# Attention's tail behind the last scores in an order of its own on free score banks; the first expert weights loaded in four column parts

## What is computed

```
x = x + mamba(layernorm(x))                      # selective scan, not changed
q, k, v = rope(norm @ Wq + bq), ctx @ Wk + bk, ctx @ Wv + bv    # 16 heads of 16, 77 keys
x = x + softmax(q k / 4) v @ Wo + bo
p = softmax(xn2 @ gate_w)                        # xn2 = layernorm(x), 8 experts
w, sel = top_k(p, 2); w = w / sum(w)
out = sum over chosen e of w_e * (up * gelu(gate)) @ down_w[e]   # gate, up = xn2 @ gate_up_w[e]
x = x + out
```

## Time and profile before

| | us |
|---|---|
| median of 3 runs | 2060.79 |
| lowest, highest | 2059.44, 2063.51 |
| the profiled execution | 2057.14 |
| its span, first to last instruction | 2055.0 |
| last scores to first gate_up matmul | 1203.5 to 1290.5 |
| expert phase from there | 764.5 |

### The profile page before, as it was taken

How to read it: one execution, slowest core, us unless ns; L and a number is a source line. 1 busy time by engine, 2 the same in 40 slices (tenths; PEclk the granted TensorE clock), 3 DMA queues, 4 the chain that set the end, 5 groups by cost and what they waited for, 6 DMA issues and landing times.

```text
span 2055.0 us, 29468 instructions
## 1 busy us (share of the span) xinstructions
PE 1867.7 (91%) x10630; PEld 1519.3 (74%) x10630; DVE 1165.8 (57%) x1760; ACT 1101.3 (54%) x2157; POOL 1099.4 (53%) x806
## 2 busy tenths in 40 slices
PE   5889999989898988878999982999999999999998
PEld 2667676767676867766666651788888888888897
DVE  4899998999999998975677753111111111111111
ACT  3898989898989998935767660111111111111111
POOL 1687878777877877844658854222222322222131
PEclk8999999999999999999999995899999999999999
DMA  4121211121121114001111013944444343444441
GB/s 118 35 63 42 63 52 63 52 58 57 44 71 42 63 43 124 18 21 46 32 42 42 26 59 110 380 137 127 127 113 144 108 149 106 125 129 110 139 152 16
DMA packets 98131, 177.21 MB, mean 86 GB/s; under 512 B 24211, under 2 KB 68627, under 8 KB 87732
## 3 DMA queue, kind: packets, MB, share of 16 engines
q1 hardware_dynamic: 82308, 156.63, 22.7%
q0 software_dynamic: 15680, 18.69, 5.5%
HBM read 152.81 MB, written 22.82 MB: 85 GB/s over the span
## 4 chain that ended last, share of the span: by engine, by line
PE 49%; ACT 4%; DVE 3%; POOL 1%; issue 1%; DMA 1%; POOLq 0%; SPq 0%; DVEq 0%; ACTq 0%
PE e_ps L1643 24%; PE e_ps L1656 12%; PE m_ps L1417 3%; PE m_ps L1347 2%; PE m_ps L1392 2%; PE m_ps L1403 1%; ACT t_probs L1005 1%; PE m_ps L1340 1%; ACT m_a_ring L369 1%; PE m_ps L1333 1%; PE e_ps L1630 1%; ACT m_bxT L381 1%; PE m_ps L684 1%; POOL slots L953 1%; PE m_ps L593 1%
## 5 line engine op out<-in xcount | busy, mean ns | idle before, releaser
L324 POOL TENSOR_TENSOR m_hc_ring<-m_h_ring,m_c_bc 128x1024 f32<-128x1024 f32 x256 | 606.0, 2373 | 128.4 <-DVE m_h_ring L485 110.1
L1643 PE MATMUL e_ps<-e_xT,e_w 128*128 128x256 f32 (+1 forms) x2560 | 501.6, 357 | 0.8 <-ACT e_xT L1571 0.8
L1643 PEld LDWEIGHTS e_ps<-e_xT,e_w 128*128 128x128 f32 x2560 | 441.3, 191 | 51.5 <-issue 1.1
L1555 POOL DMA_INDIRECT out<-e_y,e_who x71 | 113.3, 1596 | 556.4 <-DVE e_y L1607 459.2
L576 PEld LDWEIGHTS m_ps<-m_ident,m_bxT 128*128 128x128 f32 x2048 | 234.9, 141 | 216.5 <-DVE m_h_ring L485 103.3
L369 ACT ACTIVATE m_a_ring<-m_delta,m_negA 128x512 f32<-128x512 f32 x512 | 366.3, 716 | 39.6 <-DVE m_h_ring L485 39.2
L576 PE MATMUL m_ps<-m_ident,m_bxT 128*128 128x128 f32 x2048 | 320.7, 280 | 67.6 <-DVE m_h_ring L485 61.7
L381 ACT ACTIVATE m_bxT<-m_uT,m_bT 128x512 f32<-128x512 f32 x512 | 364.6, 712 | 0.0
L1598 DVE TENSOR_TENSOR e_hT<-e_gact,e_ps 128x512 f32<-128x512 f32 x142 | 97.6, 687 | 459.7 <-ACT e_gact L1580 459.7
L485 DVE TENSOR_TENSOR_SCAN m_h_ring<-m_a_ring,m_carry,m_ps 128x512 f32<-128x512 f32 x256 | 317.4, 1271 | 27.6 <-ACT m_a_ring L369 13.5
L485 DVE TENSOR_TENSOR_SCAN m_h_ring<-m_a_ring,m_ps 128x512 f32<-128x512 f32 x256 | 304.3, 1210 | 35.7 <-ACT m_a_ring L369 12.4
(11 more groups left out here) (192 smaller groups left out, 2070.2 us busy)
## 6 DMA issues: line engine op xcount, KB each, us to landing
e_w<-in_gate_up_w SPq DMA_DIRECT2D x80, 1024.0 KB, 6.8
m_c_bc<-c_rows SPq DMA_DIRECT2D x32, 1024.0 KB, 5.9
e_w<-in_down_w SPq DMA_DIRECT2D x8, 1024.0 KB, 8.1
m_x_in<-in_x SPq DMA_DIRECT2D x8, 512.0 KB, 5.6
m_x_res<-in_x SPq DMA_DIRECT2D x8, 512.0 KB, 6.8
x<-m_x_res SPq DMA_DIRECT2D x8, 512.0 KB, 2.9
t_xa<-x SPq DMA_DIRECT2D x8, 512.0 KB, 4.6
out<-t_xa SPq DMA_DIRECT2D x8, 512.0 KB, 2.9
```

The costliest lines, as they stand in the source:

```text
L324: p.tensor_tensor(hc_ring[:, k % HC, :, :], h_ring[:, n % 2, e:e + 2, :], c_bc[:, n, :].unsqueeze(1).to_broadcast([P, 2, CT]), ALU.mult).t ...
L1555: nc.gpsimd.indirect_dma_start(out=out, out_offset=bass.IndirectOffsetOnAxis(ap=who[:, tile:tile + 1], axis=0), in_=y[:, s % 2, i, :], in_ ...
L1643: last = t.matmul(gu_bank(s, g, which)[:, f * wide:(f + 1) * wide], w1[s % W1_RING][:, c, lo:lo + P], xT[:, s % 2, c, 0:wide], start=(c == ...
```

## The change

There are three edits.

1. Slots 64 to 95 are gone. In their place each engine has a function `drain`, called once, which lists the rest of attention in a written order. C5, C6, C7 are the last three chunks, L the last half. Jobs no longer share the job bank there: the last half's O goes to bank 0, OUT(7) to banks 1 and 5, NT to banks 2 and 3, LG(6) to bank 4, LG(7) to bank 1, RK(6) and RK(7) to banks 6 and 7. New semaphores `late_nt`, `late_out`, `late_lg` count their emptying.
2. On DVE the sums of the last two tiles are made one slot earlier, at the slot's head.
3. `W1_AHEAD` is gone. SP loads of the first weights only the columns of group 0 when `tables` is there (two DMAs of 128 x 2 x 256, in runs of 1 KB), and the three other groups and then step 1 after the first gather has landed. PE waits for each part in front of its group.

```diff
+        def drain():
+            normalise(TOTAL - 1)
+            for n in range(TOTAL - SCATTER_AT - C5 * HT + HT, 2 * TI):
+                scatter(C5 - 1, n)
+            for c in (C5, C6, C7):
+                for n in range(2 * TI):
+                    scatter(c, n)
...
+        def norm_turned(c, i):
+            act.wait_ge(nt_done, KD * c + i + 1)
+            if i == 0:
+                act.wait_ge(lg_done, c)
+            a.activation(xn2T[:, i, :], ps[:, LATE_NT_BANK[c][i], :], ACT.Copy).then_inc(late_nt, 1)
+
+        def drain():
+            L = HALVES - 1
+            turned(L - 1, 4)
+            head_out(L - 1)
+            turned(L, 0)
+            root(rstd2, ln2, log2, C6, rstd2_ready)
+            turned(L, 1)
+            gap_root(C5)
+            turned(L, 2)
+            normed(C6)
+            turned(L, 3)
+            turned(L, 4)
+            head_out(L)
+            norm_turned(C6, 0)
+            norm_turned(C6, 1)
+            root(rstd2, ln2, log2, C7, rstd2_ready)
+            normed(C7)
+            norm_turned(C7, 0)
+            gap_root(C6)
+            norm_turned(C7, 1)
+            gap_root(C7)
...
+        def drain():
+            shift(C6, nmr2, mv2, rstd2, rstd2_ready, nmr2_ready)
+            choose(C5, 2)
+            choose(C5, 3)
+            share_out(C5)
+            place(C5)
+            projected(C7, 0)
+            projected(C7, 1)
+            dve.wait_ge(late_out, 2)
+            measured(C7)
+            logits(C6)
+            choose(C6, 0)
+            shift(C7, nmr2, mv2, rstd2, rstd2_ready, nmr2_ready)
+            for part in range(1, 4):
+                choose(C6, part)
+            share_out(C6)
+            place(C6)
+            logits(C7)
+            for part in range(4):
+                choose(C7, part)
+            share_out(C7)
+            place(C7)
+            list_steps()
...
-            if 0 <= g - 1 < TOTAL:
+            if 0 <= g - 1 < TOTAL - 2:
                 recip(g - 1)
             if 0 <= g + 1 < TOTAL:
                 maxima(g + 1)
+            if g >= TOTAL - 2:
+                recip(g)
...
+        def late_nt_job(c, i):
+            pe.wait_ge(xn2_ready, TI * c + TI)
+            if c == C6:
+                pe.wait_ge(exp_done, TOTAL)
+            else:
+                pe.wait_ge(late_nt, 2 - i)
+            turned(lambda j: xn2s[:, c % 2, j, i * P:(i + 1) * P], nt_done, ps[:, LATE_NT_BANK[c][i], :])
...
+        def drain():
+            L = HALVES - 1
+            turn(L - 1, 4)
+            times_v(L - 1, 3)
+            times_v(L - 1, 4)
+            turn(L, 0)
+            turn(L, 1)
+            times_v(L, 0)
+            job("RK", C5, 0)
+            turn(L, 2)
+            times_v(L, 1)
+            turn(L, 3)
+            times_v(L, 2)
+            turn(L, 4)
+            times_v(L, 3)
+            times_v(L, 4)
+            late_nt_job(C6, 0)
+            late_out_job(0)
+            late_out_job(1)
+            late_nt_job(C6, 1)
+            late_lg_job(C6)
+            late_nt_job(C7, 0)
+            late_nt_job(C7, 1)
+            pe.wait_ge(tr_evac, UNITS * HALVES)
+            ranks(C6)
+            late_lg_job(C7)
+            ranks(C7)
...
         sp.wait_ge(tabled, 3)
-        for r in range(W1_AHEAD):
-            weights.load_w1(sp, r)
+        weights.load_w1_part(sp, 0)
         sp.wait_ge(blanked, 16 * 3)
...
+    def load_w1_part(sp, g):
+        e = sp.value_load(tables[0:1, 0, 0:1], min_val=0, max_val=E - 1)
+        n = F2 // 2 // W1_PARTS
+        for c in range(KD):
+            sp.dma_start(
+                w1[0][:, c, :].rearrange("p (w f) -> p w f", w=2)[:, :, g * n:(g + 1) * n],
+                gate_up_w[bass.ds(e, 1), c * P:(c + 1) * P, :].rearrange("a p (w f) -> (a p) w f", w=2)[:, :, g * n:(g + 1) * n]
+            ).then_inc(w1_part[g], 16)
...
             for s in range(STEPS):
-                if s >= W1_AHEAD:
+                if s == 0:
+                    sp.wait_ge(x_loaded[0], 16 * loads_of[0])
+                    for g in range(1, W1_PARTS):
+                        weights.load_w1_part(sp, g)
+                else:
                     if s >= W1_RING:
                         sp.wait_ge(gu_done, first_group[s - W1_RING + 1])
                     weights.load_w1(sp, s)
...
-                pe.wait_ge(w1_loaded[s % W1_RING], 16 * KD * (s // W1_RING + 1))
+                if s:
+                    pe.wait_ge(w1_loaded[s % W1_RING], 16 * KD * w1_loads_of[s])
+                else:
+                    pe.wait_ge(w1_part[0], 16 * KD)
                 pe.wait_ge(xT_ready, s + 1)
                 gate_up(s, 0)
...
                 for g in range(1, groups_of[s]):
+                    if s == 0:
+                        pe.wait_ge(w1_part[g], 16 * KD)
                     gate_up(s, g)
```

More of the change, by code:

```diff
@@ L1248, in list_steps, with measured, projected, logits @@
             v.tensor_scalar(tables[:, 2, :], eid[:], 16.0, 16.0, ALU.mult, ALU.add).then_inc(tabled, 1)
+        def measured(c):
+            for i in range(TI):
+                measure(c, i, stats2, ln2)
+            spread(c, stats2, mv2, rstd2, ln2)
+        def projected(c, i):
+            dve.wait_ge(out_done, 2 * c + i + 1)
+            dve.wait_ge(bo_added, c + 1)
+            x = xa[c % X_RING][:, 2 * i:2 * i + 2, :]
+            v.tensor_tensor(x, ps[:, LATE_OUT_BANK[i], :].rearrange("p (i d) -> p i d", d=DM), x,
+                            ALU.add).then_inc(late_out, 1)
+        def logits(c):
+            dve.wait_ge(lg_done, c + 1)
+            v.tensor_copy(lg[:].rearrange("p e i -> p i e"),
+                          ps[:, LATE_LG_BANK[c], 0:TI * E].rearrange("p (i e) -> p i e", e=E)).then_inc(late_lg, 1)
+        def drain():
[21 more added lines that the diff above has]
+            list_steps()
         def slot(g):
+            if g == TOTAL:
+                return drain()
             c, q = g // HT, g % HT
@@ L1295, in slot @@
                 wait_emptied(dve, "OUT", c - 1, 1)
-                for i in range(TI):
-                    measure(c - 1, i, stats2, ln2)
-                spread(c - 1, stats2, mv2, rstd2, ln2)
+                measured(c - 1)
             for part in range(4):
@@ L1346, in projected, with logits, ranks @@
                 for m in range(KD):
-                    last = t.matmul(job_bank[:, n * DM:(n + 1) * DM], src(m)[:, tile * P:(tile + 1) * P],
+                    last = t.matmul(bank[:, n * DM:(n + 1) * DM], src(m)[:, tile * P:(tile + 1) * P],
                                     w[:, m, :], start=(m == 0), stop=(m == KD - 1))
             last.then_inc(done, 1)
+        def logits(bank):
+            for j in range(TI):
+                for m in range(KD):
+                    last = t.matmul(bank[:, j * E:(j + 1) * E], xn2T[:, m, j * P:(j + 1) * P], gw_sb[:, m, :],
+                                    start=(m == 0), stop=(m == KD - 1))
+            last.then_inc(lg_done, 1)
+        def ranks(c):
+            pe.wait_ge(chosen, c + 1)
+            bank, flat = rank_bank(c), upto[:].rearrange("p e i -> p (e i)")
+            t.matmul(bank[:, 0:E * TI], rank_w[:, 1, :], flat, start=True, stop=False)
+            t.matmul(bank[:, 0:E * TI], rank_w[:, 0, :], both[:].rearrange("p e i -> p (e i)"),
+                     start=False, stop=True)
+            t.matmul(bank[:, E * TI:E * TI + E], rank_w[:, 1, :], upto[:, :, TI - 1],
+                     start=True, stop=True).then_inc(rk_done, 1)
         def job(kind, c, i):
@@ L1370, in job @@
                 wait_emptied(pe, "NT", c, 1)
[L1371 to L1383 removed]
+                logits(job_bank)
+            if kind == "RK":
+                ranks(c)
         def scores(g):
@@ L1457, in expert_weights @@
     w1_loaded = [sem(f"e_w1_loaded{i}") for i in range(W1_RING)]
+    w1_part = [sem(f"e_w1_part{i}") for i in range(W1_PARTS)]
     w2_loaded = sem("e_w2_loaded")
```

106 lines of the change are left out of this document (68 added, 38 removed).

## The result

The changed kernel takes 2039.12 us (median of 4 runs, 2037.27 to 2042.75) against 2060.11 (2058.39 to 2063.51) beside it on the same chip: ratio 0.9898, 95% interval 0.9879 to 0.9918, some 21 us or 1.0% faster. A repeat gave 2042.44 and 2059.96, ratio 0.991 (0.9896 to 0.9923). The profiled execution has a span of 2038.0 us (before 2055.0) and an own time of 2040.1 (before 2057.14). The gain between the two profiled executions is thus 17.0 us, and it can be followed row by row. One execution of the kernel before, beside the later runs e10 and e7, was in a slower state (2097.63 us) and is left out everywhere.

The account below looks back on a forecast made before the run. PE works without a gap for the last 765 us, so the chain of waits up to the first gate_up matmul counts. 12.0 + 4.05 + 0.6 + 2.9 = 19.6 us off 2060.8 gives 2041.2, range 2036.5 to 2049.5.

Parts of the forecast that it names:

- k: Later weight parts and step 1's weights, now issued late: arrive before PE needs them, cost nil, bounds 0 and 3 us.
- rival of two steps at half speed: First expert steps: waits for weight parts keep PE at 1.2 GHz, two steps give 2084 us; chance 0.02.
- a to d: Attention tail: last normalise 3.9 us earlier, transposes 2.1, last half's O copied out 8.2, OUT(7) 9.3.
- b: Transposes of half 15: PE, busy with products until 1212.4, starts them only 2.1 us earlier.
- c: Last half's sets and products: despite PE waits of 1.2 and 0.7 us, O is copied out 8.2 us earlier.
- e: LG(6) ahead of chunk 7's shift: costs 1.4 us, shift at 1230.5, ACT's normalise ends 9.5 us earlier.
- f: NT(7) to RK(6): separate banks cut 3.57 us to 0.9 to 1.8; `place(6)` 12.0 us earlier, bounds 8 and 13.
- g: Sixteen Pool scatters: same 1.27 us each, nothing added, so the last one starts 12.0 us earlier, at 1256.0.
- h: Last scatter's landing: 2.7 us instead of 6.75 without the 4 MB of loads; gain 4.05 us, bounds 3.5 and 4.5.
- i: Meta load and barrier: Pool starts 4.65 us after the load instead of 5.3; gain 0.6 us, bounds 0 and 0.9.
- j: First gather of tokens: lands without weight loads beside it, instead of 5.85 us; gain 2.9 us, bounds 2 and 3.1.
- rival of small parts one after another: First weight parts: six loads each take their own 2.7 us, w1(1) some 8 us late, 2049 us; chance 0.05.

Follow-up runs that it names:

- e10: Changed kernel with VectorE's shift of chunk 7 ahead of chunk 6's logits and part 0 of the weights loaded behind the barrier: 2036.10 us, ratio 0.9898.
- e7: As e10, plus ScalarE's square root for chunk 6 ahead of its copy of O: 2035.82 us, ratio 0.9896.
- e3: Changed kernel with the second edit undone, VectorE summing the last two probability tiles at their slots' ends: 2045.66 us, single run.
- e1: Changed kernel's new attention tail, but weights of steps 0 and 1 loaded as before (four 1 MB DMAs): 2045.27 us, ratio 0.9933 to the kernel before.
- e4: Changed kernel with part 0 of the first weights loaded behind the barrier, not ahead of the wait for the scatters: 2037.46 us, ratio 0.9898.
- e8: Changed kernel without parts: step 0's two 1 MB loads ahead of the records, step 1's behind the first gather: 2040.25 us, ratio 0.9911.
- e5: Changed kernel with VectorE's shift for chunk 7 ahead of the copy of chunk 6's logits and first choose step: 2039.02 us, single run.
- e9: Changed kernel with both sets of chunk 7's transposes put through one bank: 2039.76 us, single run.
- e2: Attention tail of the kernel before, with the first expert weights in four parts: 2050.85 us, ratio 0.9963 to the kernel before.
- e6: Changed kernel with ScalarE's square root for chunk 6 ahead of its copy-out of half 14's O: 2039.02 us, single run.

## Why the prediction was right, and where not

2041.2 was forecast with a range of 2036.5 to 2049.5, and 2039.12 came. On the axis of the profiled execution 2037.5 was forecast and 2040.1 came, 2.6 us of gain less. That the median agrees better is luck: the medians' difference was 21.0 us once and 17.5 in the repeat. By the prediction's own signs of being wrong it is a near thing: the last scatter starts 10.9 us earlier, where 11 to 13 was asked, and lands in about 5.1 us, where anything over 5 was to count against it. The sum of the lower bounds there (13.5) leaves out the 3 us that *k* allows; with them it is 10.5. The rival of two steps at half speed adds to 2083, not 2084. Step by step:

- *a to d* hold to 0.2 us (to 0.3 counted from the last scores, which start 0.25 us earlier in this trace): last normalise 1209.19 (forecast 1209.4), transposes 1212.22 (1212.4), RK(5) 1215.74 (1215.8), last product ended 1222.15 (1222.1), OUT(7) 1226.55 (1226.5). But the working of *b* leaves out nearly half of what the second edit brings. By e3 (one trace) the earlier sums are worth 2.06 us directly and 1.8 more while PE keeps 2.4 GHz. The text took full speed from c on, which came true, and argued from the 2.85 us stop of before; but it gave no price to the second edit's part in keeping that stop short.
- *e*: the shift came at 1231.10, forecast 1230.5. 0.45 of that is this execution's: in e1, e4 and e8 it stands at 28.62 from the last scores, here at 29.07, since ACT copied NT(6,1) 0.26 us behind PE instead of 0.04 and LG(6) took 2.13 us instead of 1.92. LG(6) ahead of the shift cost 1.0 (e5), forecast 1.4.
- *f*: `place(6)` ended at 1237.62, forecast 1236.7, 11.1 us earlier instead of 12.0. The level did fall, though ahead of the stop that was to bring it, and the slow case came: RK(6) 1.76 us behind NT(7), where 0.9 to 1.8 was given and the middle taken. e9 confirms what the banks are worth.
- *g*: from the end of `place(6)` to the last scatter 19.5 us, before 19.35. Right.
- *h* is the step that failed: "issued at about 1253, and is gone before". It was issued from 1256.45, beside the scatter, and instead of 4.05 us the term gave 1.69. e4 shows that the mechanism was right: with nothing beside it the scatter lands in about 2.8 us. The time of issue was wrong twice. `tables` is there at 1254.0, not at 1252, since `place(7)` ends at 1245.8 and not at 1244; and SP took 2.5 us from there to its first issue, where the text had 1, and 2.9 for the two DMAs. Nor would the part have been gone: where it was issued 2.1 to 2.5 us ahead of the last scatter (e2, e3, e9) it took 4.4 to 5.2 us to land, and the way from scatter to meta load was 5.60, 4.30 and 4.00 us, against 3.2 to 3.6 with nothing there. The Trainium skill's rule cited there ("DMA: Bandwidth & Descriptors", Queues, rings and completion order: turns packet by packet), read as a protection of the scatter, isn't borne out: about 2.8 us of landing with nothing on SP's queue (e4), 3.2 to 5.1 with 0.5 MB (e9 and after the ends), 6.3 with 2 MB (e8), 6.8 and 7.0 with 4 MB (before, e1).
- *i* gave 0.94 (forecast 0.6), *j* 2.88 (2.9), *k* nothing, as forecast. For the third edit that is 5.5 us, and e2 alone gave 5.71.
- Not in the sum, and not the change's: the first 16 gate_up matmuls took 0.57 us less, since the level rose earlier in them. In the two repeats it is the other way round (5.32 before, 5.96 after).
- The rival of small parts one after another didn't come: the six parts, issued 1.2 us apart, landed in 2.9 to 3.5 us each, and step 1's two loads behind them in 5.1 to 7.1. The Trainium skill's rule that goes with it ("DMA: Bandwidth & Descriptors", Bandwidth: 1 MiB or more; the fixed cost of about 2 us stands in its section Anatomy of one DMA — SWDGE (gpsimd) path) had w1(1) at about 1295, an estimate. That would have stopped PE at 1290.2, where step 1 begins (48 of 64 matmuls of 13.81 us behind 1279.82). There is no such wait.

## What to carry to other kernels

In these runs a short transfer on the critical path paid for the loads in flight beside it, though they were on another queue: place big loads by when they are in flight, and read when they are really issued, not when their wait is satisfied. In a tail the banks of finished work are free, and here one emptying taken out of a chain of short steps was worth 1.0 us (e9). An idle time of PE can cost twice, once as such and once through the clock behind it (2.06 and 1.8 us in e3); read the granted clock behind each stop, since a fall also came without a long one.

## What the runs showed of the hardware that was not expected

- Issuing is not free for strided pieces: six part loads of 128 x 2 x 256 with their register work took SP 5.8 to 7.15 us, 1.0 to 1.2 each. Two whole loads of 128 x 2048 took 0.87.
- An order of issues can move by itself: between two traces of the unchanged kernel SP's weight loads moved by 5.7 us against the work around them. With them the way from scatter to meta load got 0.8 us shorter, the meta load's landing 4.3 longer and the gather's 1.0.
- Single instructions come late with no wait that the trace names, and they do so together. In seven traces of the new tail ACT's copy of NT(6,1) follows PE by 0.03 or 0.04 us, in after, its repeat and e5 by 0.22 to 0.28, in e6 by 1.16. These four are also the ones in which SP takes 2.5 to 3.7 us from `tables` to its first issue and 2.9 for part 0's two DMAs; in e3 and e9, with the same instructions of SP, it takes 1.0 and 1.4. Why is open. A difference of 1 us in one trace is not a finding without a second trace.
